# Layer-1 attention of a two-layer block: the order in which groups of 4, 3, 2 and 1 key tiles are worked off

## The reference, cut to what matters

```python
h = _rms(x, ln_w)
q = (h @ wq).reshape(B, S, NHEADS, HEAD_DIM)      # 32 heads of 64
k = (h @ wk).reshape(B, S, KVHEADS, HEAD_DIM)     # 8 heads of 64
v = (h @ wv).reshape(B, S, KVHEADS, HEAD_DIM)
q, k = _rope(q, k)
scores = einsum('bqhd,bkhd->bhqk', q, k) / sqrt(HEAD_DIM)
scores = where(causal, scores, -1e+30)
attn = softmax(scores, -1)
o = einsum('bhqk,bkhd->bqhd', attn, v)
x = x + o.reshape(B, S, NHEADS * HEAD_DIM) @ wo
```

## Time and profile before

| | |
|---|---|
| median of 3 executions | 4737.59 us |
| lowest and highest | 4718.32, 4739.15 us |
| the profiled execution, its own time | 4729.31 us |
| its span, first to last instruction | 4727.6 us |
| mean granted TensorE clock | 0.921 |
| PE, DVE, ACT, POOL busy over the span | 85%, 69%, 42%, 30% |
| the changed stage (attention of layer 1) | about 2499 to 4230 us |

### The profile page before, as it was taken

How to read it: one execution, slowest core, us unless ns; L and a number is a source line. 1 busy time by engine, 2 the same in 40 slices (tenths; PEclk the granted TensorE clock), 3 DMA queues, 4 the chain that set the end, 5 groups by cost and what they waited for, 6 DMA issues and landing times.

```text
span 4727.6 us, 79751 instructions
## 1 busy us (share of the span) xinstructions
PE 4014.4 (85%) x26879; PEld 2405.9 (51%) x26879; DVE 3260.9 (69%) x9228; ACT 2008.0 (42%) x4657; POOL 1440.3 (30%) x1227
## 2 busy tenths in 40 slices
PE   6788888888888896996776889898989889869995
PEld 3444444444444444773453444444444444438995
DVE  7877878878787782555654576868677776764555
ACT  1244435353444453321223455555555555444442
POOL 0000000000000002332105556556554655554553
PEclk6889989898999998998898899999999999989998
DMA  4122121221221205861115811111121111135666
GB/s 118 20 33 39 28 43 28 38 38 31 39 32 27 33 15 171 260 201 48 39 71 103 90 48 48 58 46 58 37 63 37 59 48 46 51 144 104 111 107 164
DMA packets 320347, 327.56 MB, mean 69 GB/s; under 512 B 160934, under 2 KB 253630, under 8 KB 318814
## 3 DMA queue, kind: packets, MB, share of 16 engines
q1 hardware_dynamic: 275898, 250.27, 20.6%
q0 software_dynamic: 39936, 70.87, 9.0%
q10 hardware_dynamic: 4112, 1.32, 0.2%
HBM read 182.60 MB, written 92.94 MB: 58 GB/s over the span
## 4 chain that ended last, share of the span: by engine, by line
PE 61%; DVE 24%; ACT 4%; issue 4%; DMA 3%; SPq 2%; POOL 2%; another core or an unknown queue 1%; ACTq 0%; DVEq 0%; POOLq 0%
PE PS L2273 6%; PE PS L2324 6%; PE PS L2793 5%; DVE a_mm L1252 5%; PE PS L2288 4%; PE PS L2337 4%; PE PS L846 4%; PE PS L2804 3%; PE PS L2308 2%; DVE PS L2604 2%; PE PS L786 2%; PE PS L813 2%; PE PS L636 2%; PE PS L1737 2%; PE PS L824 2%
## 5 line engine op out<-in xcount | busy, mean ns | idle before, releaser
L1252 DVE TENSOR_REDUCE a_mm<-PS 128x4 f32<-128x512 f32 (+3 forms) x960 | 603.7, 649 | 246.7 <-PE PS L790 220.9
L983 ACT ACTIVATE a_PT<-PS 128x512 f32<-128x512 f32 x896 | 512.1, 601 | 595.3 <-PE PS L824 398.1
L2678 POOL TENSOR_TENSOR d_ef<-d_ef,d_soft 128x768 f32<-128x768 f32 (+3 forms) x512 | 639.6, 1259 | 353.8 <-DVE d_soft L2613 351.8
L2385 ACT ACTIVATE d_ef<-PS,d_soft 128x128 f32<-128x128 f32 (+3 forms) x1024 | 530.9, 525 | 383.6 <-DVE d_soft L2613 337.4
L2604 DVE CUSTOM_DVE_ANT_0 PS<-PS,d_cmask 128x128 f32<-128x128 f32 (+3 forms) x1024 | 481.4, 511 | 264.5 <-PE PS L2308 224.9
L1438 POOL DMA_INDIRECT list<-a_tok,slots x64 | 62.5, 976 | 1581.3 <-ACT a_PT L983 1331.2
L2288 PE MATMUL PS<-W 64*128 64x128 f32 (+3 forms) x2048 | 421.4, 489 | 85.7 <-ACT d_ef L2385 67.0
L2308 PEld LDWEIGHTS PS<-ident,d_ef 64*128 64x128 f32 x5120 | 221.4, 143 | 224.9 <-issue 95.6
L2396 ACT ACTIVATE d_tf<-PS 128x512 f32<-128x512 f32 (+1 forms) x384 | 201.8, 525 | 315.5 <-PE PS L2308 287.4
L2324 PE MATMUL PS<-d_tf,W 128*64 128x512 f32 x1280 | 327.7, 644 | 5.5 <-DVE d_tf L2622 4.9
L2308 PE MATMUL PS<-ident,d_ef 64*128 64x64 f32 x5120 | 237.2, 229 | 109.4 <-ACT d_tf L2396 37.4
(11 more groups left out here) (385 smaller groups left out, 7728.5 us busy)
## 6 DMA issues: line engine op xcount, KB each, us to landing
W<-W SPq DMA_DIRECT2D x768, 64.0 KB, 2.0
W<-in_exp SPq DMA_DIRECT2D x96, 384.0 KB
e_xg<-xrow SPq DMA_DIRECT2D x144, 132.5 KB
a_Q<-scr SPq DMA_DIRECT2D x384, 32.0 KB
yrow<-bc_ob SPq DMA_DIRECT2D x48, 256.0 KB
W<-in_exp SPq DMA_DIRECT2D x16, 768.0 KB, 10.1
scr<-a_qsp SPq DMA_DIRECT2D x24, 384.0 KB, 3.0
acc<-in_zero POOLq DMA_DIRECT2D x34, 256.0 KB, 12.0
```

The source lines that it names most:

```text
L983: e.activation(PT[:, 4 * (n % 2) + q4, :], RS.of(("exp", n, q4))[:, :], ACT.Exp, scale=S0).then_inc(act.sem, act.mark(("exp", n, q4)))
L1252: e.tensor_reduce(mm[:, i % 2, kind, c:c + len(gs)], RP.of(("top", b, u, kind, gs[0]))[:, 0:len(gs) * n].rearrange("p (g k) -> p g k", g=l ...
L2385: e.activation(ef[:, n % 7, r, 0:nk], S.of(("exp", n))[:, r, 0:nk], ACT.Exp, scale=-1.0, bias=nm[:, n % 7, r:r + 1], accum_out=zz[:, n % 7 ...
L2678: e.tensor_tensor(ef[:, n % 7, :, 0:nk], ef[:, n % 7, :, 0:nk], zr[:, n % 7, :].unsqueeze(2).to_broadcast([128, 2, nk]), ALU.mult).then_in ...
```

## The change

`unit` no longer counts the query tile up. A list `order` of the eight groups of a block gives (hh, i) in turn, so the numbers of key tiles of the groups are 4, 1, 4, 1, 3, 2, 3, 2. Each J is now complete when its later group is: `last(J)` is its last unit, which is unit 5 of the block for i = 3, 7 for i = 0, 13 for i = 2 and 15 for i = 1. The J are numbered in that order. `ready` puts `times` at `last(J) + 7`, `out_proj` 2 steps later and `collect` 4 steps later. In positions of a block: `times` at 12, 14, 4, 6; `out_proj` at 14, 16, 6, 8; `collect` at 16, 18, 8, 10 (those from 16 on lie in the next block, 16 being its position 0). The ring `tf` keeps its 12 tiles, and a tile is skipped where a pair would wrap around; the waits for a free tile are counted anew. The `square` pieces move to positions 1, 3, 9 and 11. The number and the shapes of all instructions stay as they were.

```diff
+            order = [(0, 3), (0, 0), (1, 3), (1, 0), (0, 2), (0, 1), (1, 2), (1, 1)]
+            finish = sorted((max(m for m, x in enumerate(order) if x[1] == i), i) for i in range(4))
+            closing = [i for _, i in finish]
 
             def unit(n):
                 b, m = n // N, n % N
-                return b, m // 16, m // 4 % 4, m // 2 % 2, m % 2
+                hh, i = order[m % 16 // 2]
+                return b, m // 16, i, hh, m % 2
+
+            def group(J, hh):
+                return 8 * (J // 4) + order.index((hh, closing[J % 4]))
+
+            def whole(g):
+                return 4 * (g // 8) + closing.index(order[g % 8][1])
+
+            def last(J):
+                return 16 * (J // 4) + 2 * finish[J % 4][0] + 1
 
             def pair(g, part):
-                nb = g // 2 % 4 + 1
+                nb = order[g % 8][1] + 1
                 return tuple(range(2 * part, min(2 * part + 2, nb)))
...
+            ready = {last(J) + 7: J for J in range(2 * N)}
...
-            late = {-22: ("x2", 0), -1: ("square", 0), 3: ("square", 1), 7: ("square", 2), 11: ("square", 3),
-                    12: ("h2root", 0), 14: ("h2", 0), 15: ("h2", 1), 16: ("HT", 0), 17: ("gate", 0),
+            late = {-22: ("x2", 0), 12: ("h2root", 0), 14: ("h2", 0), 15: ("h2", 1), 16: ("HT", 0), 17: ("gate", 0),
...
+            late.update((last(J) - 4, ("square", closing[J])) for J in range(4))
...
-                    if n >= 10 and n % 4 == 2 and (n - 10) // 4 < 2 * N:
-                        times((n - 10) // 4)
-                    if n >= 12 and n % 4 == 0 and (n - 12) // 4 < 2 * N:
-                        out_proj((n - 12) // 4)
-                    if n >= 14 and n % 4 == 2 and (n - 14) // 4 < 2 * N:
-                        collect((n - 14) // 4)
+                    if n in ready:
+                        times(ready[n])
+                    if n - 2 in ready:
+                        out_proj(ready[n - 2])
+                    if n - 4 in ready:
+                        collect(ready[n - 4])
...
-                    if i == 0 and f == 0:
+                    if i == order[0][1] and f == 0:
...
-                        c = place[g, js[-1]]
-                        if c >= 12:
-                            e.wait_ge(pe.sem, pe.at(("pv", tiles[c - 12][0] // 2)))
+                        old = [whole(tiles[place[g, j] - 12][0]) for j in js if place[g, j] >= 12]
+                        if old:
+                            e.wait_ge(pe.sem, pe.at(("pv", max(old))))
```

More of the change, by code:

```diff
@@ L2083, in phase_d @@
             N = 64
-            tiles = [(g, j) for g in range(4 * N) for j in range(g // 2 % 4 + 1)]
-            place = {t: c for c, t in enumerate(tiles)}
+            order = [(0, 3), (0, 0), (1, 3), (1, 0), (0, 2), (0, 1), (1, 2), (1, 1)]
+            finish = sorted((max(m for m, x in enumerate(order) if x[1] == i), i) for i in range(4))
+            closing = [i for _, i in finish]
             def unit(n):
                 b, m = n // N, n % N
-                return b, m // 16, m // 4 % 4, m // 2 % 2, m % 2
+                hh, i = order[m % 16 // 2]
[6 more added lines that the diff above has]
+                return 16 * (J // 4) + 2 * finish[J % 4][0] + 1
             def pair(g, part):
-                nb = g // 2 % 4 + 1
+                nb = order[g % 8][1] + 1
                 return tuple(range(2 * part, min(2 * part + 2, nb)))
+            tiles, place = [], {}
+            for g in range(4 * N):
+                for part in range(2):
+                    js = pair(g, part)
+                    if len(js) == 2 and len(tiles) % 12 == 11:
+                        tiles.append(tiles[-1])
+                    for j in js:
+                        place[g, j] = len(tiles)
+                        tiles.append((g, j))
+            ready = {last(J) + 7: J for J in range(2 * N)}
             def halves(p, js):
@@ L2181, in after @@
                 def after(piece, k, b):
-                    if piece == "square" and k == 3 and b == 7:
+                    if piece == "square" and k == closing[3] and b == 7:
                         e.wait_ge(pe.sem, pe.at(("pv", 127)))
@@ L2313, in times @@
                 def times(J):
-                    b, hp, i, _, _ = unit(4 * J)
+                    b, hp, i, _, _ = unit(last(J))
                     p, old = TX.take(act, ("oT", J))
@@ L2319, in times @@
                     for u, who in enumerate((act, dve)):
-                        e.wait_ge(who.sem, who.at(("tf", 2 * J + 1, i // 2, u)))
+                        e.wait_ge(who.sem, who.at(("tf", last(J) // 2, i // 2, u)))
                     for j in range(i + 1):
@@ L2324, in times @@
                             e.matmul(p[64 * hh:64 * hh + 64, :], vt[:, b % 2, j, 64 * kv:64 * kv + 64],
-                                     tf[:, place[2 * J + hh, j] % 12, :], start=(j == 0), stop=(j == i)
+                                     tf[:, place[group(J, hh), j] % 12, :], start=(j == 0), stop=(j == i)
                                      ).then_inc(pe.sem, pe.mark(("pv", J)))
                 def out_proj(J):
-                    b, hp, i, _, _ = unit(4 * J)
+                    b, hp, i, _, _ = unit(last(J))
                     if J:
@@ L2465, in after @@
                         moments(y[:, k, :], k)
-                        if k == 3:
+                        if k == closing[3]:
                             square_mean("h2var", b)
@@ L2625, in collect @@
                 def collect(J):
-                    b, _, i, _, _ = unit(4 * J)
+                    b, _, i, _, _ = unit(last(J))
                     y = y2[:, b % 2, i, :]
@@ L2675, in scale @@
                     new(n)
-                    nk = 128 * (n // 4 % 4) + 128
+                    nk = 128 * unit(n)[2] + 128
                     e.wait_ge(dve.sem, dve.at(("inv", n)))
```

## The result

The changed kernel takes **4966.8 us** (median of four executions, 4956.31 to 4972.48), the kernel before 4732.24 us beside it (4718.32 to 4739.15): a ratio of 1.0497, 95% interval 1.0465 to 1.0529. It is slower by 5%, inside the range, on the side forecast, 75 us above the forecast number. The two profiled executions have spans of 4954.6 and 4727.6 us, 227.0 us apart.

A forecast was written before the change was run, and what follows sets the result against it. PE was taken as the busiest engine, standing still 22.1 us a batch, mostly for exponentials and weight copies. The steps sum to 155 us on 4729.3, 4884; with the median 8 us above, 4892 us, range 4810 to 4980.

The forecast's parts named there:

- Step 1: At positions 0 and 8, `out_proj` makes PE wait for DVE's addition: 1.92 and 1.65 us a stop, 111 us slower.
- Step 2: The same wait where DVE is late, at positions 16, 32 and 40: 2.5 us a batch, 18 us slower.
- Steps 3, 4 and 5: Exponential waits at positions 9 to 12, +13 us; positions 0 to 4, -2 us; loaded stretches otherwise, 0.
- step 4: Positions 0 to 4: unit 3's scores wait 1.35 us for exponentials of a four-tile unit; net -2 us.
- Step 6: PE's granted clock in the attention falls a little because of the new stops: 20 us slower, bounds 0 and 100.
- Step 7: First batch, where POOL stands behind its DMAs: new PE stops fall partly into that time, -5 us.
- The clock gives way: Rival: the clock loss in PE's work reaches its upper end, 80 us more, 4972 us; chance 0.12.
- The new stops replace old ones: Rival: stops at `out_proj` partly take the place of PE's waits for exponentials, 61 us less, 4831 us; chance 0.15.
- Faster: Rival: even groups halve DVE's and POOL's backlog in loaded blocks and hide stops there, -47 us, 4690 us; chance 0.04.
- That the change does nothing: Rival: the addition is done before PE reaches the projection, or stops and gains cancel, 4738 us; chance 0.03.

The follow-up runs named there:

- one kind of stop left: Changed kernel with only the output projection of i = 0 one step later, the stop at position 8 staying: 4772.94 us, 1.0183 of the kernel before.
- waits in the old order: Kernel before, old group order, with `collect` of i = 2 and 3 two steps later so the projection waits: 4830.84 us, 1.0323 of the kernel before.
- side work later: Changed kernel with `h2` and what follows it in `late` moved one to three steps later: 5004.82 us, 1.0677 of the kernel before.

## Why the prediction was right in sign and short in size

- **Step 1 holds.** The line that had no idle time has it, the releaser is DVE's addition, it happens 48 times in six batches, and a plain stop is 2.08 and 1.82 us where 1.92 and 1.65 were taken from the earlier trace rows. The excess is 0.10 us between the reciprocal and the addition and 0.06 from the addition's end to PE's start, both in the timeline of position 48. In a middle batch it is 15.6 us against 14.3. The experiments with the projection later show that nothing else makes the 5%.
- **Step 2 was mis-sized.** It took 2.5 us a batch for the stops where DVE is late, on the ground that most is repaid. The excess at 16, 32 and 40 is 1.95, 1.89 and 1.10 us over the plain stops, 4.9 us a batch. DVE is less late than the 3.4 us that were read from the earlier trace rows (1.4 us in the timeline of position 16), but nothing of it is seen to be repaid: all other waits together did not fall in these batches. Steps 1 and 2 forecast 129 us together. The group of the projection in the page has 159.6 us of idle time after and 0.9 before.
- **Steps 3, 4 and 5 hold as a sum.** The forecast for them was 11 us. In the six batches standing still rose by 125.1 us, of which 123.3 are the stops, so all else changed by 2; the three were not measured one by one. With the stops taken away the order is at 0.998 to 1.001 of before. The wait before the scores of unit 3 (step 4) is there in blocks 2 to 4 of batch 3, 1.22, 0.98 and 1.23 us against a forecast of 1.35, and missing in the first.
- **Step 6 failed; it is the term that the forecast lacks.** It took 20 us, near the lower end, because the stops are short and have dense work around them, like the fourth block at 1.00. That block is now at 0.91. PE's busy time rose by 85.2 us on the page, and in the middle batches by 12.5 us each, just the upper bound worked out from the earlier trace rows. One reading was wrong before the run: the clock of the earlier trace rows is not lowest where PE stood still most densely, since block 1 stood still for 6.7 of 54.4 us (12%) at 0.94 and block 2 for 7.0 of 53.4 (13%) at 0.97. What counted was not how dense the work around a stop is. The clock roughly followed the standing still: 0.97, 0.96, 0.94, 0.92 and 0.88 where PE stood still for 10%, 14%, 16%, 18% and 19% of six batches (projection later, one kind of stop left, waits in the old order, the changed kernel once more, side work later). Other runs lie off that line (the order 1, 4, 1, 4 with 12% at 0.95, the filled stops with 15% at 0.94), and the earlier stage in the earlier trace rows does so most (12.5% at 0.91), so the share alone does not set it. Half of the price lies on the eight matmuls right behind the stops.
- **The Trainium skill** (TensorE: Matmul & The Clock Gate, section "Loop structure matters more than you think") gave 0 for this step. In its example the next matmuls follow at once; here they wait for DVE, so it does not cover this case, and the 0 that the prediction took from it is refuted. The section "A second HAM failure mode: psum-queue depth-cycling" of the same page speaks of the clock swinging where PE idles briefly and often between groups of matmuls. The trace agrees, 0.97 to 0.91.
- **Step 7 was mis-sized.** It took -5 us off the first batch. That batch lost 9 us (240 instead of 231), where a middle one lost 33.3. There the stops do replace other waits: they come to 14.9 us, and PE's waits for POOL's scales fell from 26.7 to 9.4.
- **The sum.** Forecast 155 on the profiled execution, measured 227.0: steps 1 and 2 short by 30, step 6 by 65, and the rest 23 lower than the 6 us forecast for it (in the middle batches it is +2, so the gain lies outside them, in the first batch among others). The misses partly cancel. **The rivals:** "The clock gives way", 4972, is within 6 us of the result; it was held at 0.12. Its mechanism is the one that came true, but so close a number is luck: the clock cost 85 us and not 100, step 2 was taken too small and the first batch too dear. "The new stops replace old ones" fell: waits for exponentials 52.1 before, 55.7 after. "Faster" fell as well: the stops stand in the loaded blocks too, and are longest there. That the change does nothing is excluded by the trace.

**Still open.** Why the clock holds behind the stops at 8 and 24 (1.82 us, after scores of three tiles) and falls behind those at 0 and 48 (2.08 us, after scores of four) was not found; length, place and the work before differ together. That the waits in the old order cost less clock (0.94) than the same number in the new one was not followed up either.

## What to carry to other kernels

When an order is changed in programs that are fixed for each engine, list for every wait across engines how many steps lie between its two ends, after the change as before. Where they fall into one step, the price is the whole way of the other engine through that step, twice a block here, and one step of distance takes it away. And where PE is the bound, price standing still twice: once as time, and once as what the clock does to the work behind it, which here was 60% of the first (75 against 125 us).

## What was not expected of the hardware

Short stops, two in a block of some 61 us and 2 to 4 us each, took the granted clock of this stage from 0.97 to 0.91. One projection shows what that means: its eight matmuls take 1.99 us in the timeline of the filled stop and 3.78 us in that of the moved side work, the ratio of the two clock levels within 5%. So a part of the price of a stop lies on the instructions behind it, which do not change in any way, and it is paid or not by stop: 1.99 us behind 1.82 us of standing still at 8, 3.02 on average behind 2.08 at 0. A projection with no stop before it costs what it did (97.2 us for 48, against 198.0 for 96 before).

Matmuls of no use made a kernel faster: 62 sets of some 1.0 us, filled into stops, gave 24 us back (4908.69 to 4884.84), though the kernel before stays far ahead of both.
